# Quadrant layout of B, C and the step sizes, and half of the token rows gathered inside the main loop

## The reference

```python
# 1 embedding: four tiers of a table, each scaled by its row ts and quantised with one scale per tier
table = concat([quantize(tw[i] * ts[i], bits=(16, 8, 6, 4)[i]) for i in range(4)])     # 50257 x 256
h = table[input_ids]
# 2 block on layernorm(h): a mixer (recurrence over 128 tokens) and an MLP 256 -> 1024 -> 256
z, u, B, C, dt = split(rms(x) @ in_proj.T, [512, 512, 16, 16, 8])
u, B, C = silu(causal_conv4([u, B, C]))
B, C = B * rsqrt(sum(B * B) + 1e-6), C * rsqrt(sum(C * C) + 1e-6)
d = softplus(dt + dt_bias)                                    # 8 heads
for t: Z = (Z + d * (u B - A * Y)) / (1 + d * d * A); Y = Y + d * Z; out = Y . C
x = x + out_proj((out + D_skip * u) * silu(z)); x = x + fc2(gelu(fc1(rms(x))))
h = h + x
# 3 linear layer in int8 on layernorm(h), with one scale for the whole tensor
h = h + int8_linear(layernorm(h))
```

## Time and profile before

| | |
|---|---|
| median of three runs | 1486.99 us (1486.4 to 1487.03) |
| the profiled execution: its time, its span | 1489.13 us, 1487.3 us |
| busy in the span: PE, DVE, POOL, ACT | 1203.7, 1205.1, 848.8, 809.2 us |
| granted TensorE clock, mean | 0.932 of full speed |
| main loop | from about 179.5 to 1431 us |

### The profile page before, as it was taken

The page is one execution under the profiler, slowest core; times in us unless marked ns, Lnnn a source line. Parts: engine busy times, 40 slices in busy tenths (PEclk is TensorE's granted clock), DMA queues, the critical chain, the costliest instruction groups (busy, mean ns, idle before and its releaser), DMA issues. The chain is left out here.

```text
span 1487.3 us, 24635 instructions
## 1 busy us (share of the span) xinstructions
PE 1203.7 (81%) x6751; PEld 794.8 (53%) x6758; DVE 1205.1 (81%) x2087; ACT 809.2 (54%) x1108; POOL 848.8 (57%) x2326
## 2 busy tenths in 40 slices
PE   0693043498989999989999989999999999998767
PEld 0352011356575656565657565656566665657444
DVE  4899833688888888888888888888898988878268
ACT  4667253355647473838383838374747465641248
POOL 7860027575757576665757575757575757570100
PEclk9999987599999999999999999999999999999889
DMA  9999300000000010101000000000000000000015
GB/s 364 407 408 425 132 18 14 15 17 16 17 14 22 9 30 0 30 2 29 7 23 12 18 16 15 16 15 16 15 16 15 16 15 16 16 17 1 0 37 189
DMA packets 33811, 91.34 MB, mean 61 GB/s; under 512 B 8973, under 2 KB 17922, under 8 KB 29298
## 3 DMA queue, kind: packets, MB, share of 16 engines
q1 hardware_dynamic: 30226, 81.32, 15.4%
q0 software_dynamic: 3072, 8.39, 1.5%
q10 hardware_dynamic: 480, 1.24, 0.2%
HBM read 81.21 MB, written 9.70 MB: 61 GB/s over the span
## 5 line engine op out<-in xcount | busy, mean ns | idle before, releaser
L739 POOL TENSOR_TENSOR stp<-Gs,X 128x32 f32<-128x32 f32 x1024 | 290.3, 284 | 266.4 <-ACT X L714 176.7
L741 POOL TENSOR_TENSOR Gs<-Gs,stp 128x32 f32<-128x32 f32 x1024 | 298.2, 291 | 80.3
L600 PE MATMUL bank<-xT,w_in 128*128 128x512 f32 (+1 forms) x576 | 266.6, 609 | 15.0 <-DVE uT L843 8.2
L1059 PE MATMUL bank<-w_fc,gl 128*128 128x256 f32 x1024 | 238.0, 380 | 13.5 <-ACT gl L1050 13.5
L1040 PE MATMUL bank<-mT,w_fc 128*128 128x512 f32 x512 | 237.9, 603 | 1.5 <-ACT mT L1028 1.5
L1059 PEld LDWEIGHTS bank<-w_fc,gl 128*128 128x128 f32 x1024 | 192.2, 190 | 78.2 <-issue 30.1
L829 ACT ACTIVATE uT<-bank,cols 128x512 f32<-128x512 f32 x64 | 49.4, 776 | 251.6 <-PE bank L600 251.6
L600 PEld LDWEIGHTS bank<-xT,w_in 128*128 128x128 f32 (+1 forms) x576 | 103.0, 186 | 139.5 <-issue 117.4
L1040 PEld LDWEIGHTS bank<-mT,w_fc 128*128 128x128 f32 x512 | 95.6, 191 | 112.4 <-issue 106.9
L944 PE MATMUL bank<-MT,utok 128*64 128x128 f32 x1024 | 111.9, 409 | 45.5 <-DVE MT L930 45.5
L843 DVE SCALAR_TENSOR_TENSOR uT<-bank,cols,uT 128x500 f32<-128x500 f32 (+1 forms) x192 | 134.4, 730 | 2.3
(11 more groups left out here) (169 smaller groups left out, 1971.1 us busy)
## 6 DMA issues: line engine op xcount, KB each, us to landing
ring<-in_table SPq DMA_DIRECT2D x32, 1536.0 KB, 21.3
d_rep<-scan_rows SPq DMA_DIRECT2D x128, 64.0 KB, 2.0
out<-res SPq DMA_DIRECT2D x16, 512.0 KB, 2.9
b_rep<-scan_rows SPq DMA_DIRECT2D x128, 32.0 KB, 1.8
c_rep<-scan_rows SPq DMA_DIRECT2D x128, 32.0 KB, 1.8
w_fc<-in_w_fc SPq DMA_DIRECT2D x2, 1024.0 KB, 8.8
w_in<-in_w_in ACTq DMA_DIRECT2D x1, 1064.0 KB
h<-in_table,ids POOLq DMA_INDIRECT x64, 10.1
```

Of the source, the lines that this page charges most:

```text
L600: last = pe.matmul(dst, w_in[:, k, c0:c1], xT[:, k, :], start=(k == 0), stop=(k == KD - 1))
L739: pool.tensor_tensor(stp[:], Gs[:, t, ::-1, :], X2[:, t, :, :], ALU.mult).then_inc(rec.sem, 1)
L741: pool.tensor_tensor(Gs[:, t + 1, :, :], Gs[:, t, :, :], stp[:], ALU.add).then_inc(rec.sem, 1)
L1059: last = pe.matmul(sbk[j // 2][:, (j % 2) * D:(j % 2 + 1) * D], gl[n % LEAD][:, j * LEN:(j + 1) * LEN], w_fc2[:, n, :], start=(n == 0 and ...
```

## The change

Two things are changed together. B, C and the step sizes of the four sequences of a group now lie on four quadrants of 32 partitions, one for each sequence, with 128 columns: `pe_small` writes them with sixteen matmuls of 32x128 instead of two of 40x512, dt is padded to 32 rows and has its own bank and tiles (`dt`, `soft`, `dd`), and all the small operations of ACT and DVE work on 128x128 instead of 32x512 or 8x512. SP's transfers carry the same bytes in pieces of 512 B. And the prologue gathers and scales only the rows of the first eight groups. The rows of groups 8 to 15 are gathered by POOL in turns 2 to 9, at the start of the turn and six groups ahead, together with each token's row of `ts` (four gathers each, into `h` and `ts_tok`), and are multiplied with it by POOL at the end of the turn. DVE computes the tier of each token in the prologue for it (`tier_id`).

```diff
-SMALL = 2 * NST + HEADS
+SMALL = 2 * NST
+EARLY = 32
+LATE_GROUP = EARLY // G
+AHEAD = 6
...
-                for b in range(SEQS):
+                for b in range(EARLY):
                     pool.indirect_dma_start(
...
-            PAIRS = SEQS // 2
+            PAIRS = EARLY // 2
...
+                dve.tensor_tensor(idf[:], ge[:, 1, :], ge[:, 2, :], ALU.add).then_inc(hot_made, 1)
+                dve.wait_ge(hot_made, 6)
+                dve.tensor_tensor(tier_id[:], idf[:], ge[:, 3, :], ALU.add)
...
+        def pool_fetch(pool, g):
+
+            n = g - LATE_GROUP
+            if n:
+                pool.wait_ge(late_scaled.sem, late_scaled.at(n - 1))
+            for j in range(G):
+                b = g * G + j
+                pool.indirect_dma_start(
+                    out=h[:, b * D:(b + 1) * D], out_offset=None, in_=a["table"],
+                    in_offset=bass.IndirectOffsetOnAxis(ap=ids[:, b:b + 1], axis=0)).then_inc(late_in.sem, 16)
+                pool.indirect_dma_start(
+                    out=ts_tok[:, j, :], out_offset=None, in_=a["ts"],
+                    in_offset=bass.IndirectOffsetOnAxis(ap=tier_id[:, b:b + 1], axis=0)).then_inc(late_in.sem, 16)
+
+        def pool_scale(pool, g):
+            pool.wait_ge(late_in.sem, late_in.at(g - LATE_GROUP))
+            pool.tensor_tensor(rows(g, 0, G), rows(g, 0, G), ts_tok[:].rearrange("p j c -> p (j c)"), ALU.mult) \
+                .then_inc(late_scaled.sem, 1)
...
-        def dve_quantise(dve, g):
+        def dve_quantise(dve, g, late=False):
+
+            if late:
+                dve.wait_ge(late_scaled.sem, late_scaled.at(g - LATE_GROUP))
...
-            project(pe, tb[0][0:SMALL, :], 2 * DIN, 2 * DIN + SMALL, small_mm.sem)
...
+            for part in range(2):
+                c0 = 2 * DIN + part * SMALL
+                for k in range(KD):
+                    for j in range(G):
+                        last = pe.matmul(tb[part][SMALL * j:SMALL * (j + 1), 0:LEN],
+                                         w_in[:, k, c0:c0 + SMALL], xT[:, k, j * LEN:(j + 1) * LEN],
+                                         start=(k == 0), stop=(k == KD - 1), skip_group_check=True)
+            last.then_inc(small_mm.sem, 1)
...
-            act.activation(bc[DT, :], ps[DT, :], ACT.Identity, bias=c("dt_bias", 0, DT)).then_inc(dt_in.sem, 1)
-            act.activation(bsq[DT, :], ps[DT, :], ACT.Abs, bias=c("dt_bias", 0, DT)).then_inc(dt_in.sem, 1)
+            act.activation(dt[:], dt_raw, ACT.Identity, bias=c("dt_bias")).then_inc(dt_in.sem, 1)
+            act.activation(soft[:], dt_raw, ACT.Abs, bias=c("dt_bias")).then_inc(dt_in.sem, 1)
...
-            pe.matmul(tb[1][:, :], norm_sum[:], bsq[BC, :], start=True, stop=True).then_inc(ss_mm.sem, 1)
+            pe.matmul(tb[1][:, LEN:2 * LEN], norm_sum[:], bsq[:], start=True, stop=True).then_inc(ss_mm.sem, 1)
...
-            dve.scalar_tensor_tensor(bcd[DT, :], bc[DT, :], 0.0, bsq[DT, :], ALU.max, ALU.add) \
+            dve.scalar_tensor_tensor(dd[:], dt[:], 0.0, soft[:], ALU.max, ALU.add) \
...
-                    sp.dma_start(d_rep[32 * head:32 * head + 32, hg, :],
-                                 scan_rows[row:row + 1, :].to_broadcast([32, TOK])).then_inc(d_in.sem, 16)
+                    row = 4 * hg + head
+                    sp.dma_start(d_rep[32 * head:32 * head + 32, hg, :].rearrange("p (j t) -> p j t", j=G),
+                                 d_rows[:, row:row + 1, :].rearrange("j r t -> r j t").to_broadcast([32, G, LEN])) \
+                        .then_inc(d_in.sem, 16)
...
-            def turn(g, first, second, third, nxt):
+            def turn(g, first, second, third, nxt, fetched=None):
                 p, m = g - 1, g - 2
+                if fetched is not None:
+                    pool_fetch(pool, fetched)
                 if third:
                     pool_residual(pool, m)
...
                 if first:
                     pool_recurrence(pool, g, range(CL // 2, CL))
+                if fetched is not None:
+                    pool_scale(pool, fetched)
...
-            turns(pool, turn)
+            turn(0, True, False, False, True)
+            turn(1, True, True, False, True)
+            for g in range(2, GROUPS - AHEAD):
+                turn(g, True, True, True, True, g + AHEAD)
+            with pool.Fori(GROUPS - AHEAD, GROUPS - 1) as g:
+                turn(g, True, True, True, True)
```

More of the change, by code:

```diff
@@ L133, in build @@
         tb, sbk, pj = bank[0:2], bank[2:4], bank[4:8]
+        ids = sb("ids", [P, SEQS], I32)
+        tier_id = sb("tier_id", [P, SEQS], I32)
         ids_in, const_in, weight_in = sem("ids_in"), sem("const_in"), sem("weight_in")
         rows_in = [sem(f"rows_in{i}") for i in range(RING)]
-        gathered = [sem(f"gathered{i}") for i in range(SEQS // GATHERS)]
+        gathered = [sem(f"gathered{i}") for i in range(EARLY // GATHERS)]
         tile_read = sem("tile_read")
@@ L414, in build @@
         lnst = sb("lnst", [P, 8, G])
-        bc = sb("bc", [SMALL, TOK])
-        bsq = sb("bsq", [SMALL, TOK])
-        nrm = sb("nrm", [2 * NST, TOK])
-        bcd = sb("bcd", [SMALL, TOK])
+        bc = sb("bc", [P, LEN])
+        bsq = sb("bsq", [P, LEN])
+        nrm = sb("nrm", [P, LEN])
+        bcd = sb("bcd", [P, LEN])
+        dt = sb("dt", [P, LEN])
+        soft = sb("soft", [P, LEN])
+        dd = sb("dd", [P, LEN])
         X2 = sb("X2", [P, CL, 2, LANES])
@@ L438, in build @@
         half = sb("half", [P, G])
+        ts_tok = sb("ts_tok", [P, G, D])
         eps5 = sb("eps5", [P, G])
@@ L1219, in dve_turn, with turn @@
         def dve_turn(dve):
-            def turn(g, first, second, third, nxt):
+            def turn(g, first, second, third, nxt, late=False):
                 p, m = g - 1, g - 2
                 if nxt:
-                    dve_quantise(dve, g + 1)
+                    dve_quantise(dve, g + 1, late)
                 if first:
@@ L1277, in dve_turn @@
             dve_rms_rows(dve, 0)
-            turns(dve, turn)
+            turn(0, True, False, False, True)
+            turn(1, True, True, False, True)
+            with dve.Fori(2, LATE_GROUP - 1) as g:
+                turn(g, True, True, True, True)
+            with dve.Fori(LATE_GROUP - 1, GROUPS - 1) as g:
+                turn(g, True, True, True, True, True)
+            turn(GROUPS - 1, True, True, True, False)
+            turn(GROUPS, False, True, True, False)
+            turn(GROUPS + 1, False, False, True, False)
         def pool_turn(pool):
-            def turn(g, first, second, third, nxt):
+            def turn(g, first, second, third, nxt, fetched=None):
                 p, m = g - 1, g - 2
+                if fetched is not None:
+                    pool_fetch(pool, fetched)
                 if third:
@@ L1598 @@
     cols["norm2"][:] = tall(f["L0_attn_norm2_w"])
-    cols["bc_tap"][0:2 * NST] = taps[DIN:]
-    cols["bc_bias"][0:2 * NST, 0] = f["L0_attn_conv_b"][DIN:]
-    cols["dt_bias"][2 * NST:SMALL, 0] = f["L0_attn_dt_bias"]
+    cols["bc_tap"][:] = np.tile(taps[DIN:], (G, 1))
+    cols["bc_bias"][:, 0] = np.tile(f["L0_attn_conv_b"][DIN:], G)
+    for j in range(G):
+        cols["dt_bias"][SMALL * j:SMALL * j + HEADS, 0] = f["L0_attn_dt_bias"]
     cols["u_tap"][:] = taps[:DIN].reshape(UT, P, TAPS).transpose(1, 0, 2).reshape(P, UT * TAPS)
```

56 lines of the change are left out of this document (27 added, 29 removed).

## The result

The changed kernel takes **1491.96 us** (median of six runs, 1491.45 to 1493.66) against 1486.7 for the kernel before on the same chip (six runs, 1484.8 to 1487.67): the ratio is 1.0039, with a 95% interval of 1.0026 to 1.0052. It is slower by 5.3 us. The forecast was slower by 26. The profiled execution took 1493.19 us, with a span of 1491.3 (1487.3 before) and a mean granted clock of 0.909 (0.932).

What follows compares the result with a forecast made beforehand. TensorE's chain sets the turn, with a GpSimd ring nearly as long. Prologue -10.5, turn 0 -2.2, turn 2 +2.6, turns 3 to 9 +36.4, turn 10 +1.5, turns 11 to 15 -1.5: +26.3, giving 1513 us; range 1476 to 1538.

Steps and rivals of the forecast that it cites:

- the clock's part: Turns with gathers: TensorE idles some 6 us before the scores, whose first half then runs at a slow clock, +1.7 us.
- Turn 2: First turn with gathers, having no product ahead of them: 76.9 - 2.6 - 71.7 = +2.6 us.
- the next E comes 0.05 + 13.37 + 30.52 later: Turn with gathers, after L1081: slack before scores, scores to VectorE's last mean, then GpSimd to the next E; turn 75.2 us.
- E: The end of GpSimd's last recurrence step in a turn, from which the forecast counts times.
- Its late result is what L899 waits for: Turns with gathers: L1069, GpSimd's first residual product, ends at E + 17.4, delaying VectorE's layer norm; L1081 ends at E + 31.3.
- TensorE's chain sets the turn. But a second ring is nearly as long: Main loop before: TensorE busy 66.57 of 71.60 us; the ring through GpSimd, residual, VectorE and scores takes 71.70.
- the ring holds this back: Turns without gathers: TensorE's 2.3 us earlier scores are limited by a GpSimd ring of 70.7; gain 1.0 at most, -0.3 taken.
- The prologue: 16 of 32 scale products leave VectorE, 10.3 us, and DMA stays hidden; -10.5 taken, bounds -9 and -12.
- Turn 0: One serial chain, shortened by the quadrant layout: 0.85 + 1.45 + 0.40 - 0.5 = -2.2 us.
- The gathers fit: Rival, start of turns 2 to 9: faster if the ring stays under about 73.5, a gather under 1.3 us; chance 0.24.
- a gather wait out a whole operation of DVE: Rival, turns with gathers: 2.3 us each, 18.4 for eight, 83.3 a turn, about 1565 us; chance 0.05.
- The column quarters: Rival, TensorE's small projection: quarters run in series, 3.5 us instead of 1.05, about 1522 us; chance 0.06.

Runs made afterwards that it cites:

- e1: Changed kernel with all 64 token rows gathered and scaled in the prologue again, only the quadrant layout staying; 1464.15 us, ratio 0.9853.
- e3: Changed kernel with GpSimd issuing the eight gathers behind the residual instead of ahead of it in turns 2 to 9; 1470.9 us, ratio 0.9894.
- e5: Kernel before (old layout, all gathers in prologue) with VectorE's four norm operations cut from 512 columns to 128; 1485.5 us, ratio 0.9988.
- e2: Changed kernel with an extra VectorE product of 384 columns ahead of each of the four norm operations; 1494.21 us, ratio 1.0051.
- e4: Changed kernel without the gathers of the tier's scales and their product, four gathers a turn staying ahead of the residual; 1492.25 us, ratio 1.0035.
- e7: Changed kernel with twelve gathers a turn in turns 2 to 9 in place of eight, the added ones never read; 1548.69 us, ratio 1.040.
- e12: e5 with TensorE's small projection also cut to 128 of 512 columns, in the old layout; 1472.04 us, ratio 0.9899.
- e8: Changed kernel with residual first, late gathers spread over turns 0 to 13 behind it, products behind three recurrence steps; 1453.69 us, ratio 0.9781.
- e9: e8 with the product of the scales moved right behind the four gathers, ahead of the recurrence; 1472.43 us, ratio 0.9894.
- e6: As e4 with two gathers a turn in place of four, the other late rows gathered in the prologue; 1468.59 us, ratio 0.9881.

## Why the prediction was right and wrong

*The sign and its reason were right*: the gathers stand ahead of the residual, and the turns with them lose more than the prologue gives. e1 and e3 show both. The price of a gather was right too (1.5 forecast, 1.46 to 1.53 measured), and so was the clock's part (the scores took 3.69). Turn 2 came out right by luck, +2.9 against +2.6: the missing product was to make it 2.6 us shorter than the other turns with gathers, and it was 0.3 shorter (74.9 and 75.2 from squares to squares), while all of these turns were shorter than forecast.

*The step that failed* is "the next E comes 0.05 + 13.37 + 30.52 later". The forecast carried POOL's 30.52 us from the means to the next E over from the earlier trace rows into every turn, though the change shortens just the DVE operations that run beside it. It measured 28.6 to 29.0 in turns 2 to 14. By the forecast's own sum that is 1.8 to 1.9 us in each of turns 3 to 9, 13 of the 22 us by which the sum was off, and it is most of what turns 10 to 15 gained beyond the forecast. e5 shows that the short norm operations are enough to shorten the stretch. How much of it reached the turns of 75.1 is not shown: e2 put 0.4 us back and they stayed as long. *Turn 1*, which the sum leaves out without a reason, gave 2.4 us. From E to E it took 65.40 us and not 67.35, and its last stretch 27.06 and not 28.99, so that here the gain is this step.

*The mechanism of the first stretch was right at eight gathers and not the whole of it.* "Its late result is what L899 waits for" gave a start of the layer norm at E + 17.4 and an addition at E + 31.3; they were 17.4 to 17.6 and 30.9. In turns 4, 5, 8 and 9 L940 did wait, for 2.47 us, and was then shut out once, as forecast. In turns 3, 6 and 7 nothing waited: L845 and L940 were shut out, one after the other, at the same price. What the forecast lacks is that this price is due with four gathers as well (e4), where no result is late; that eight gathers cost neither more nor less is where the two prices happen to meet, and e4 and e7 tell them apart.

*"TensorE's chain sets the turn. But a second ring is nearly as long"* held, as far as e5 and e12 show the two chains. But "the ring holds this back", with a gain of 1.0 at most and -0.3 taken for a turn without gathers, came from the same 30.52. Measured, such a turn gains 1.0 on average in turns 11 to 14 of the changed kernel and 1.2 in e1.

*The prologue* was -12.2: 10.3 as worked out for the scale products, and 1.9 because DVE waited less for ACT between its first fold and its last, 13.9 us and not 15.8. The folds themselves took as long as before, 118.0 and 118.1 us in all. Behind the gathers DVE folded without a gap, 56.01 us for 16 tiles, so DMA did not become the limit there. *Turn 0* gave 4.9 and not 2.2. Up to the first recurrence step it was 2.9, with a dearer landing of `d_rep` as forecast (2.7 us in e1, against 2.0 in the earlier trace rows); the other 2.1 are in the recurrence with its norm factors, 47.4 us and not 49.5 from its first step to its last, which the forecast had left as they were.

*The rivals.* "The gathers fit" did not come about: the turns stayed at 75.1, above its threshold of 73.5. By an estimate from the result, break-even lay near 74.4 (75.1 less the 5.3 us spread over eight turns). Nor does a gather wait out a whole operation of DVE, which had a chance of 0.05: they stand 1.46 to 1.53 us from one to the next, and not 2.3. The column quarters did not run in series. No run shows how the forecast's 1.05 us for the small projection in the new layout comes about, it was an estimate; the changed kernel's 32 passes took 1.08 us, at a granted clock of 1.00, where one after the other they were put at 3.5.

## What to carry to other kernels

When an engine's operations shut another engine out, ask for each of them not how long it takes but what the other engine has to do at that moment: a product of the residual cost the turn nothing in DVE's gap and 2.2 us beside the keys and the layer norm (3.43 us where L845 usually takes 1.05, 3.75 where the layer norm takes 1.67), and a product of the scales nothing beside a reciprocal (6.54 us with it and without) and 1.0 us beside the layer norm (2.65 and not 1.67). A duration read from the trace of before is only good for after if what runs beside it stays the same: L661 took 2.23 us beside L1069 and 0.68 without it. A wait has to be looked for in every turn: that of the layer norm shows in four of seven. And with two chains of nearly equal length, shortening one shows nothing (e5) until the other is shortened too (e12); work put into idle time belongs behind whatever the other engines wait for (e3, e8).

## What the runs showed of the hardware

The second stretch goes with the granted clock, and not in proportion to the delay. With the addition at E + 26.4 to 27.3 the stretch to the norm factors is 13.9 to 14.1 us in five of thirteen turns of e1, at a mean granted clock of 0.76 to 0.88, and 15.5 to 16.1 in the others, at 0.57 to 0.61. With it at 27.4 (e9) it is 15.55 in turns 4 to 12, at 0.57 to 0.58; at 28.6 (e6) it is 14.7 in five of seven turns, at 0.65 to 0.67, and 16.9 in two, at 0.52; at 36.1 (e7) it is 17.2, at 0.50. So 1.0 us of delay cost 1.4 us a turn in e9, and 2.1 us of it cost 1.3 in five turns of e6 and 4.2 in the other two, against e1's mean of 70.5. In the changed kernel PE idled 4.78 us ahead of scores that took 3.69, in the kernel before 0.91 ahead of scores of 2.01. I did not find what decides in e1 which turn is the fast one.

A gather's issue took 0.95 us with DVE idle (L548 at 617.77 in the changed kernel, where DVE idles from 616.27 to 618.75; the same for the gathers at 12.05 and 13.30 of the kernel before, where it idles from 10.82 to 15.51) and 1.77 and 1.74 beside the keys' first products in that turn, L803 to L809; but beside later products of the same kind it took 0.94 to 1.13. What makes the difference stays open.
